# Deformable convolution ahead of attention: offset convolution and Z on 64-row tiles, in two pairs of images

## The reference, cut to what matters

```python
om = conv3x3(x, offset_w) + offset_b          # 27 outputs a position
offset, mask = om[..., :18], sigmoid(om[..., 18:])
pos_y = clip(base_y + inner_y + offset_y, 0, 17)   # for each of 9 taps
pos_x = clip(base_x + inner_x + offset_x, 0, 17)
value = bilinear(pad_x, pos_y, pos_x) * mask       # per tap, 64 channels
out = einsum(value, dcn_weight)                    # sum over taps and channels
```

## Time and profile before

| | us |
|---|---|
| median of 3 runs | 384.88 (384.58 to 385.8) |
| the profiled execution, its own time | 385.77 |
| its span | 384.0 |
| TensorE busy in it | 364.0 |

### The profile page before, as it was taken

The page is one execution under the profiler, slowest core; times in us unless marked ns, Lnnn a source line. Parts: engine busy times, 40 slices in busy tenths (PEclk is TensorE's granted clock), DMA queues, the critical chain, the costliest instruction groups (busy, mean ns, idle before and its releaser), DMA issues.

```text
span 384.0 us, 15270 instructions
## 1 busy us (share of the span) xinstructions
PE 364.0 (95%) x5880; PEld 194.9 (51%) x5880; DVE 239.1 (62%) x1234; ACT 225.2 (59%) x1073; POOL 56.5 (15%) x124
## 2 busy tenths in 40 slices
PE   8999999899999999999999999999999999999996
PEld 2576765454554455445645554554455455543332
DVE  3388665645656666666666666757675666664443
ACT  2496664615854785477548655864686478544342
POOL 3101001311211220122011211211121112110000
PEclk9999999999999999999999999999999999999999
DMA  8000000000000000000000000000000000000000
GB/s 253 15 2 5 12 15 15 14 2 3 3 4 3 7 3 2 3 7 4 3 3 5 5 2 5 4 4 3 5 4 3 3 7 3 3 2 6 3 2 4
DMA packets 4806, 4.33 MB, mean 11 GB/s; under 512 B 3837, under 2 KB 4286, under 8 KB 4734
## 3 DMA queue, kind: packets, MB, share of 16 engines
q1 hardware_dynamic: 4432, 2.84, 2.7%
q10 hardware_dynamic: 302, 0.52, 0.4%
HBM read 2.57 MB, written 0.26 MB: 7 GB/s over the span
## 4 chain that ended last, share of the span: by engine, by line
PE 67%; DVE 15%; ACT 11%; issue 6%; DMA 1%; DVEq 0%; ACTq 0%
PE bank L758 18%; PE bank L394 12%; PE bank L546 9%; DVE bank L1290 6%; PE bank L563 5%; DVE H L1300 5%; ACT bank L934 4%; ACT bank L927 4%; PE bank L461 4%; PE bank L584 4%; PE bank L451 3%; PE bank L422 2%; ACT E L859 2%; PE bank L655 1%; PE bank L689 1%
## 5 line engine op out<-in xcount | busy, mean ns | idle before, releaser
L394 PE MATMUL bank<-FB 128*128 128x512 bf16 (+3 forms) x490 | 141.1, 369 | 1.2 <-DVE FB L956 1.2
L758 PEld LDWEIGHTS bank<-H,VW 64*32 64x32 f32 x3060 | 52.1, 106 | 104.9 <-DVE H L1300 103.1
L927 ACT ACTIVATE bank<-bank 64x8 f32<-64x8 f32 x256 | 37.6, 147 | 87.8 <-PE bank L758 84.6
L758 PE MATMUL bank<-H,VW 64*32 64x4 f32 x3060 | 74.3, 176 | 11.9 <-DVE H L1300 1.5
L1290 DVE TENSOR_TENSOR_SCAN bank<-bank,SU 64x12 f32<-64x12 f32 x256 | 48.5, 189 | 49.9 <-ACT bank L927 47.3
L1300 DVE SCALAR_TENSOR_TENSOR H<-TO,bank 64x4 f32<-64x4 f32 x256 | 40.7, 159 | 44.8 <-ACT bank L934 34.1
L394 PEld LDWEIGHTS bank<-FB 128*128 128x128 bf16 x490 | 38.7, 99 | 22.1 <-issue 4.2
L371 POOL TENSOR_SCALAR E<-E,rinv 128x256 f32<-128x256 f32 x62 | 29.8, 480 | 126.1 <-DVE rinv L1092 126.1
L934 ACT ACTIVATE bank<-bank 64x4 f32<-64x4 f32 x256 | 38.4, 150 | 15.9
L931 ACT ACTIVATE TO<-bank 64x4 f32<-64x4 f32 x256 | 43.8, 171 | 6.3
L1284 DVE SCALAR_TENSOR_TENSOR SU<-H,bank 64x4 f32<-64x4 f32 x256 | 41.2, 161 | 9.1
(11 more groups left out here) (123 smaller groups left out, 311.1 us busy)
## 6 DMA issues: line engine op xcount, KB each, us to landing
AW<-in_attn_w SPq DMA_DIRECT2D x1, 768.5 KB, 8.2
DW<-in_dcn_w SPq DMA_DIRECT2D x1, 576.0 KB, 6.7
X<-in_x_fm SPq DMA_DIRECT2D x1, 256.0 KB, 3.3
X<-in_x_fm ACTq DMA_DIRECT2D x1, 256.0 KB, 5.5
T<-T0T SPq DMA_DIRECT2D x16, 16.0 KB, 1.8
Y<-YT SPq DMA_DIRECT2D x16, 16.0 KB, 1.8
out_dram<-OUT SPq DMA_DIRECT2D x8, 32.0 KB, 1.4
CW<-in_conv_w SPq DMA_DIRECT2D x1, 243.5 KB, 4.0
```

Source lines behind the costliest of these rows:

```text
L394: nc.tensor.matmul(idle[:, 0:n], FB[:, 0:P], FB[:, 0:n], start=True, stop=True)
L758: mm = nc.tensor.matmul(gate_out(m, gate, r, slice(B * s, B * (s + 1))), VW[0:C, gate, r], H[0:C, (STEPS * m + s - 1) % RING, :], start=Fa ...
L927: nc.scalar.activation(GT[:, :, 1:3].rearrange("p b g -> p g b"), b_cell[m % 2][0:C, 0:2 * P].rearrange("p (g s b) -> p g s b", g=2, b=B)[ ...
```

## The change

The offset convolution is made for one pair of images at a time, `offsets(0)` and `offsets(1)`. Each is 18 matmuls of 64 rows (one image), 32 columns of weights and 256 columns of input, on four tiles of the array: two images by even and odd taps. The sum of the even and odd taps and the transpose become one matmul with a matrix of ones in the right places (`partials`, loaded with the constants): `offsets_turned(j)`. The bias is added by ScalarE for the first pair and by VectorE (`offsets_out`) for the second.

Z is made by matmuls of 64 rows, two images at once on the two row halves of the array and into two banks; DW is loaded without its zeros, half the size. Only the first pair's Z, `z(0)` to `z(3)`, is made before the sampling. `z(4)` to `z(7)` stand after the gathers of batches 1 to 4, and their copies stand among ScalarE's copies of AT in batches 2 to 5. `offsets_turned(1)` stands in batch 1, and VectorE takes the second pair's positions ahead of group 6.

The hats of image 0 are made in two pieces, the first SOONER = 3 taps and then the rest. POS, MK and HAT are laid out anew, so that positions are one operation a pair and the hats of a piece are one operation for rows and columns together. The second fill has 2048 columns instead of 4096. PSUM banks are handed out anew, with the waits that go with it.

```diff
-COLS_GROUPS = 4096
+COLS_GROUPS = 2048
+DISTANCES_AT = 1
+SOONER = 3
+OM_TILE = 32
-        b_misc, b_om, b_omt = banks[0], banks[1], banks[2]
-        b_z = banks[3:8] + banks[0:1]
-        b_at = banks[1:3] + banks[0:1]
+        b_misc, b_om, b_omt = banks[0], (banks[1], banks[7]), (banks[2], banks[6])
+        b_z = [(banks[i], banks[j]) for i, j in ((3, 4), (5, 6), (0, 1), (3, 4), (5, 3), (6, 7), (5, 3), (6, 7))]
+        b_at = [banks[2], banks[0], banks[1]]
...
+            def offsets(j):
+                pe.wait_ge(xn_done, j + 1)
+                for t in range(TAPS):
+                    dy, dx = t // 3, t % 3
+                    for h in range(2):
+                        r = slice(C * h, C * (h + 1))
+                        q = OM_TILE * (2 * h + t % 2)
+                        mm = nc.tensor.matmul(b_om[j][q:q + OM_TILE, 0:N].rearrange("p (y x) -> p y x", y=SIDE),
+                                              OW[r, t, :], XN[r, j, dy:dy + SIDE, dx:dx + SIDE],
+                                              start=(t < 2), stop=(t >= TAPS - 2))
+                mm.then_inc(om_mm, 1)
+            def offsets_turned(j):
+                pe.wait_ge(om_sb, j + 1)
+                if j == 1:
+                    pe.wait_ge(z_sb, 4)
+                for h in range(HALVES):
+                    mm = nc.tensor.matmul(b_omt[j][:, OFFS2 * h:OFFS2 * (h + 1)], OM[:, j, P * h:P * (h + 1)], partials,
+                                          start=True, stop=True)
+                mm.then_inc(omt_done, 1)
             def z(i):
+                j, pt, m = i // 4, i // 2 % 2, i % 2
+                if i == 3:
+                    pe.wait_ge(z_sb, 2)
+                elif i == 5:
+                    pe.wait_ge(pos_done, 2)
+                    pe.wait_ge(mask_act, 2)
+                elif i >= 6:
+                    pe.wait_ge(z_sb, 2 * (i - 1))
+                for h in range(2):
+                    r = slice(C * h, C * (h + 1))
+                    nc.tensor.matmul(b_z[i][h][:, 0:ZC], XC[r, j, P * pt:P * (pt + 1)], DW[r, ZC * m:ZC * (m + 1)],
                                      start=True, stop=True).then_inc(z_mm, 1)
+            offsets(0)
             z(0)
+            offsets_turned(0)
+            for i in range(1, 4):
                 z(i)
+            offsets(1)
...
             def turn(g):
-                    pe.wait_ge(dist, 1)
-                if g == 2:
-                    pe.wait_ge(z_sb, 4 * B)
+                    pe.wait_ge(pos_done, 1)
+                    pe.wait_ge(mask_act, 1)
+                elif g < TURNS:
+                    pe.wait_ge(z_sb, 6)
             def gather(g):
+                if k == 0:
+                    pe.wait_ge(z_sb, (8, 14, 16, 16)[b])
             def tokens(b):
                 if b == 0:
-                    pe.wait_ge(z_sb, 4 * B)
+                    pe.wait_ge(z_sb, 14)
...
+                if j == 1:
+                    offsets_turned(1)
                 if j >= 1:
                     for g in range(BATCH * (j - 1), BATCH * j):
                         gather(g)
+                if 1 <= j <= 4:
+                    z(3 + j)
...
+            nc.scalar.activation(OM[:, 0, :], b_om[0][:, 0:N], ACT.Identity, bias=OB).then_inc(om_sb, 1)
+            z_out(0, 0)
+            z_out(0, 1)
+            masks(0)
+            z_out(1, 0)
+            hats_abs(0, slice(0, SOONER), 1)
+            hats_relu(0, slice(0, SOONER), 1)
+            z_out(1, 1)
+            hats_abs(0, slice(SOONER, TAPS), 2)
+            hats_relu(0, slice(SOONER, TAPS), 2)
+            z_out(2, 0)
+            z_out(2, 1)
...
+                if j == 0 and g < 2:
+                    z_out(3, g)
+                elif 2 <= j <= 5 and g % BATCH < 2:
+                    z_out(2 + j, g % BATCH)
+                if g == 2 * BATCH - 1:
+                    masks(1)
...
+            def offsets_out():
+                nc.vector.tensor_scalar(OM[:, 1, :], b_om[1][:, 0:N], OB, None, ALU.add).then_inc(om_sb, 1)
+            def positions(j):
+                dve.wait_ge(omt_done, j + 1)
+                nc.vector.tensor_tensor(POS[:, j, :, :, :], src, base[:, :, None, :].to_broadcast([P, HALVES, 2, 2 * TAPS]),
+                                        ALU.add).then_inc(pos_done, 1)
+                dve.wait_ge(pos_done, j + 1)
+                link(nc.vector.tensor_scalar(pos, pos, 0.0, float(SIDE + 1), ALU.max, ALU.min))
...
-            distances(0)
-            distances(1)
+            positions(0)
+            distances(0, slice(0, SOONER))
+            distances(0, slice(SOONER, TAPS))
+            mask_scaled(0)
             for g, (b, k) in enumerate(GROUPS):
                 if k == 0:
-                    masked(b)
-                if k == 3 and b + 2 < B:
-                    distances(b + 2)
+                    masked(b, slice(0, TAPS if b else SOONER), b + 2 if b else 1)
+                elif g == SOONER - 1:
+                    masked(b, slice(SOONER, TAPS), 2)
+                if g == SOONER:
+                    distances(1, slice(0, TAPS))
+                elif g == SOONER + 1:
+                    offsets_out()
+                elif g == 2 * SOONER:
+                    positions(1)
+                elif g == TAPS:
+                    mask_scaled(1)
+                elif k == DISTANCES_AT and 1 <= b < B - 1:
+                    distances(b + 1, slice(0, TAPS))
```

More of the change, by code:

```diff
@@ L146, in hybrid_kernel @@
         XC = sb("XC", [P, 2, N])
[L147 to L150, removed]
+        OM = sb("OM", [P, 2, N])
+        POS = sb("POS", [P, 2, HALVES, 2, 2 * TAPS])
+        MK = sb("MK", [P, 2, HALVES, 2, TAPS])
+        HAT = sb("HAT", [P, B, HALVES, TAPS, 2, SIDE])
         A = sb("A", [P, SLOTS, HALVES, N])
@@ L795, in _ @@
                                ).then_inc(xc_done, 1)
[L797 to L802, removed]
-            act.wait_ge(om_mm, 1)
-            for j in range(2):
-                nc.scalar.activation(OM[:, j, :], b_om[0:OFFS2, N * j:N * (j + 1)], ACT.Identity, bias=OB
-                                     ).then_inc(om_low, 1)
@@ L808, in _ @@
[L808 to L831, removed]
+            def z_out(i, h):
+                j, pt, m = i // 4, i // 2 % 2, i % 2
+                act.wait_ge(z_mm, 2 * i + h + 1)
+                nc.scalar.copy(Z[:, pt, 2 * j + h, :, :].rearrange("p k f -> p (k f)")[:, ZC * m:ZC * (m + 1)],
+                               b_z[i][h][:, 0:ZC]).then_inc(z_sb, 1)
@@ new lines, in masks, with hats_abs @@
+            def masks(j):
+                act.wait_ge(pos_done, j + 1)
+                nc.scalar.activation(MK[:, j, :, :, :],
+                                     b_omt[j][:, 0:HALVES * OFFS2].rearrange("p (h b o) -> p h b o", h=HALVES, b=2)
+                                     [:, :, :, 2 * TAPS:OFFS], ACT.Tanh, scale=0.5).then_inc(mask_act, 1)
+            def hats_abs(b, taps, n):
+                v = HAT[:, b, :, taps, :, :].rearrange("p h k d v -> p h (k d v)")
+                act.wait_ge(dist, n)
+                nc.scalar.activation(v, v, ACT.Abs).then_inc(hat_abs, 1)
@@ new lines, in hats_relu @@
+            def hats_relu(b, taps, n):
+                v = HAT[:, b, :, taps, :, :].rearrange("p h k d v -> p h (k d v)")
+                act.wait_ge(hat_abs, n)
+                nc.scalar.activation(v, v, ACT.Relu, bias=1.0, scale=-1.0).then_inc(hat_act, 1)
+            act.wait_ge(ld_cw, 16)
+            act.wait_ge(om_mm, 1)
+            nc.scalar.activation(OM[:, 0, :], b_om[0][:, 0:N], ACT.Identity, bias=OB).then_inc(om_sb, 1)
+            z_out(0, 0)
+            z_out(0, 1)
+            masks(0)
@@ L984, in _ @@
                                         gmv[:, j, 0:1], grs[:, j, :], ALU.subtract, ALU.mult).then_inc(xn_done, 1)
[L986 to L989, removed]
             dve.wait_ge(ld_k, 16)
[L992 to L1000, removed]
@@ new lines, in mask_scaled, with distances @@
+            def mask_scaled(j):
+                dve.wait_ge(mask_act, j + 1)
+                mk = MK[:, j, :, :, :].rearrange("p h b k -> p (h b k)")
+                link(nc.vector.tensor_scalar(mk, mk, 0.5, 0.5, ALU.mult, ALU.add))
+            def distances(b, taps):
+                pos = POS[:, b // 2, :, b % 2, 2 * taps.start:2 * taps.stop]
+                to = [P, HALVES, 2 * (taps.stop - taps.start), SIDE]
+                nc.vector.tensor_tensor(HAT[:, b, :, taps, :, :].rearrange("p h k d v -> p h (k d) v"),
+                                        pos[:, :, :, None].to_broadcast(to),
+                                        grid[:, None, None, :].to_broadcast(to), ALU.subtract).then_inc(dist, 1)
@@ L1021, in sampled, with masked @@
+            def masked(b, taps, n):
+                dve.wait_ge(hat_act, n)
+                v = HAT[:, b, :, taps, 0, :]
+                m = MK[:, b // 2, :, b % 2, taps]
+                link(nc.vector.tensor_tensor(v, v, m[:, :, :, None].to_broadcast([P, HALVES, taps.stop - taps.start, SIDE]),
```

(4 more changed lines are left out.)

76 lines of the change are left out of this document (22 added, 54 removed).

## The result

The changed kernel took 386.16 us (median of 11 executions, 384.55 to 388.0), the kernel before, run beside it, 384.58 (11 executions, 384.54 to 385.8). The ratio over all these executions is 1.0033, with a 95% interval of 1.0019 to 1.0046 (that of the two medians is 1.0041): slower by a third of a per cent or a little more, where 1.5 us of gain were forecast, and outside the range given.

A forecast was written before the change was run, and what follows sets the result against it. TensorE, 95% busy, was taken to bound the early chain. Of 4.25 us gained by turn(6), 1.38, 1.0 and 0.69 were lost and 0.3 regained: 1.5 us off 384.88 gave 383.4 us, range 382.2 to 385.7.

The forecast's parts named there:

- convolution at 8.40: Start of the first pair's offset convolution on TensorE, after the shorter fills and the XN writes: forecast at 8.44 us.
- first A: First product A of the sampling on VectorE: forecast to start at 14.57 us, against 20.38 before.
- turn(6): TensorE's turn after gathers 0 to 2 and z(4): forecast at 22.85 us against 27.1, 4.25 us gained so far.
- a stand of 0.99 us before `tokens(0)`: TensorE waiting for ScalarE's copy of the second half of z(6): forecast to cost about 1.0 us.
- `channels(0)`: TensorE's step after the first image's token chain: forecast at 36.5 us against 38.00, the whole 1.5 us gain.
- changes of shape: Z within the sampling: each z costs 0.69 us, some 0.2 of it for changing tile shape at either end.
- the tiles do not run four at once: Rival on the offset convolution: it is 1.75 us longer on the path, 385.1 us, about no change; chance 0.07.
- no wait for z(6): Rival at `tokens(0)`: quicker copies, or the token chain setting `channels`, return up to 1 us, 382.4 us; chance 0.07.
- fall among the turns: Rival: the clock falls during turns alone, 16.5 to 20.3 us, costing 1.75 us, 385.1 us; chance 0.06.
- Nothing behind is touched, so the end moves by it.: After `channels`, LSTM included: the program's end was to come earlier by the full 1.5 us.
- Four of eight fills go, so TensorE is free at about 7.9: Second fill ahead of the offset convolution: TensorE was to be free at about 7.9 us instead of 9.7.
- the clock rises later: Rival: all of `offsets(0)` runs at the lower clock, finishing 1.5 us later; no gain, 384.9 us; chance 0.20.

The follow-up runs named there:

- first experiment: The changed kernel with one of VectorE's six small memsets at the start given to GpSimd: 384.93 us, ratio 1.0003 to the kernel before.
- eighth experiments: The kernel before with one small memset more on VectorE at the start: 386.19 us for the execution, LSTM stretch 294.4 us.
- fourth: The changed kernel with both copies of a second pair's Z ahead of the batch's first AT copy on ScalarE: 384.18 us, ratio 0.9979 to the kernel before.
- ninth experiment: The kernel before with the second fill at 2048 columns instead of 4096, nothing else: 386.40 us, ratio 1.0021 to the kernel before.
- third experiment: The changed kernel with the second fill at 4096 columns again: 384.81 us, ratio 1.0006 to the kernel before.

## Why the prediction was wrong

**What held.** The front, term by term: convolution at 8.40 (8.44), seen by ScalarE at about 11.4 (11.35), first A at 14.81 (14.57), turn(6) at 23.12 (22.85), turn(12) at 30.31 (30.05), a stand of 0.99 us before `tokens(0)` (1.0), `channels(0)` at 36.56 (36.5). From the first A on the terms come 0.24 to 0.27 late, and only the last one makes up for it, for which the sum has no reason: that `channels(0)` agrees to 0.06 is in part luck. The row of the first A:

```profile
14.81 1.29 DVE L1162 TENSOR_TENSOR A<-HAT 128x512 f32<-128x512 f32 x2
```

Four tiles do run at once: 36 passes in 2.35 us. A z costs 0.69 from its start to the next turn (22.44 to 23.12 and the three after it). z(1) to z(3), with no other shape between them, take 1.66 together (12.57 to 14.23), 0.48 for each after the first if the first costs 0.69 as well; so some 0.2 of the 0.69 goes to the changes of shape, as the prediction had it. Nothing of the rivals "the tiles do not run four at once" and "no wait for z(6)" came true, and in the profiled execution the clock did not fall among the turns: it stands at 1.00 from 16 to 21 us.

**What failed, first step: "Nothing behind is touched, so the end moves by it."** The LSTM's instructions are the same, but their places in VectorE's stream are not. One record more ahead of them puts H, on which every step ends, at four of the places where VectorE starts late, and other operations (the scan, O's copy, a reciprocal) at more. That cost 1.07 us of a lead of 1.37. The prediction had no term for it: it took instructions that are not edited to keep their time. Moving one memset gave it back (292.80), and adding one to the kernel before took it there too. What makes every 128th record late is not seen directly. The page of the profile lists transfers of queue 14, kind "instruction", and one begins at 131.16 us, 0.68 after the late H. It is so all through: in the traces of the kernel before, the changed one and the first and eighth experiments, each of the 14 records with the remainder 63 from number 191 on is followed, 0.55 to 0.93 us after its start, by an 8 KB transfer of this queue. The transfers go with the places, then; but they begin after the late instruction, so it isn't for them that it waits. The Trainium skill ("Runtime: NRT & Kernel Launch", "Instruction fetch mechanics") says that an engine's instruction memory is a small FIFO refilled in blocks while the engine runs, 256 instructions each. The trace agrees on blocks, with one transfer to 128 records of VectorE and not to 256.

**Second step: "Four of eight fills go, so TensorE is free at about 7.9".** That was worked out for an execution in which the level rises at about 9.7, because the profiled one was such. Most executions are not: eight of the 11 of before lie at 384.5 to 384.9, three at 385.6 to 385.8, and the traces with eight fills and an early rise have them done in 1.89 us. There four fills end near 6.9, and in part of these executions the level, already up, falls again at the convolution (the first experiment's trace), in others not (the fourth's and ninth's). The rivals had the clock rising late or falling among the turns; that it could fall after an early rise I had not seen, although the row that shows the fills at 0.446 each and that at 0.215 hold what is needed to ask. The rival "the clock rises later" had the right price, 1.5 us for a convolution at the lower level throughout (measured 1.7, 4.04 against 2.35), by another way to it. In the first experiment the five executions at 0.995 and 0.996 are 1.8 to 2.0 us slower than its fastest. The profiled execution of the changed kernel (385.46) is one in which the level rose late and wasn't lost; five of its 11 executions have 0.991 to 0.995, at 386.2 us and more, and put the median 0.7 us above it.

**The account.** With the level kept and an early rise, the front is ahead by 1.27 us (`channels(0)` at 35.62 in the third experiment, at 36.89 in the kernel before with a memset more, where the level was up early as well). Less 1.07 that leaves 0.2, and the third experiment measured 1.0006 (0.9991 to 1.002), no change. With the memset moved it is 0.9978, with the stand removed as well 0.9940. The first experiment alone left the clock as it was: 1.0003.

**Open.** Why the level rises early in one execution and late in the next; what decides, after an early rise and the short fill, whether it is kept (fourth and ninth experiment) or lost (first); whether the level was ever lost among the turns; what the slowest single executions are (387.45 at 0.999, 387.56 at 1.000); and what it is in VectorE that makes every 128th record late.

## What to carry to other kernels

Where a long loop is bound by a chain through a single engine, an edit ahead of the loop also moves the loop's instructions within that engine's stream; look for single iterations that are late with nothing to wait for, and move one instruction to another engine before judging the edit. Work out a fill, or anything that keeps TensorE busy, for both levels of the clock: fills counted in columns last half as long once the level is up, and TensorE then stands idle just before the work begins. Here the cure was more columns; spreading the same ones out did nothing. And one profiled execution shows one course of the clock; where the executions fall into groups, sort them by their mean clock before you explain a median.

## What the runs showed of the hardware that was not expected

H started about 0.21 us late where it fell on one of the places 128 apart in VectorE's stream. Such places cost the LSTM 1.05 to 1.07 us more when they fell on H and other operations that are waited for than when they fell on SU, which then started 0.05 us late; each was followed by an 8 KB transfer of queue 14. The granted clock fell to 0.50 after 1.24 us without work that followed 1.02 us of fills, in an execution in which it had been 1.00 just before; in two others it stayed at the upper level through 1.34 and 1.57 us without work behind the same fills, and in all 30 executions of the changed kernel's variants with twice the fills no mean clock was under 0.997. A stretch of turns alone, 16.5 to 20.5 us, ran at a granted clock of 1.00 after the level was up.
